# Full-height count products, a three-pass down product, and a reordered opening in a fused embedding, attention and expert kernel

## The reference, cut to what matters

```python
h = concat([cls, patches(x) @ W.T + b]) + pos          # 16 images: 197 rows of 192
h = concat([h, txt], axis=1)                           # + 128 text rows: S = 325
n = layernorm(h); q, k, v = split(n @ W_qkv + b_qkv)
h = h + ((q @ k.T) / sqrt(192) * decay_mask) @ v       # causal 0.99**(i-j), no softmax
n = layernorm(h)                                       # T = 16*325 = 5200 tokens
sig = sigmoid(n @ Wg.T); idx = top_k(sig + e_bias, 6)  # 128 experts, 6 per token
w = 2.5 * sig[idx] / sum(sig[idx])
for e in experts:                                      # the first 192 tokens of each
    g, u = split(n[tokens_e] @ W_gate_up[e])           # 192 -> 2 x 464
    routed[tokens_e] += (silu(g) * u) @ W_down[e] * w  # 464 -> 192
shared = silu(n @ Wsg) * (n @ Wsu) @ Wsd               # 192 -> 928 -> 192, all tokens
out = h + routed + shared
```

## Time and profile before

| | |
|---|---|
| three runs | 699.82, 701.12, 701.90 us; median 701.12 |
| profiled execution | 699.24 us, span 697.4 us |
| busy, share of the span | TensorE 97%, its weight load 91%, VectorE 67%, ScalarE 48%, POOL 29% |
| chain that ended last | TensorE 80%, VectorE 10%, issue 4% |
| images 0 to 15, with the opening | about 0 to 270 us |
| counts and chunks ahead | about 270 to 319 us |
| ten pairs of experts | 318.7 to 672.6 us, 35.4 us each |

### The profile page before, as it was taken

One profiled execution on the slowest core, in us unless ns is written; L12 is line 12 of the kernel. 1 busy time (PEld: TensorE's weight loads), 2 busy tenths in 40 slices (PEclk: granted clock), 3 DMA queues, 4 the chain that ended last, 5 costly groups with the idle time before them and its releaser, 6 DMA issues.

```text
span 697.4 us, 16667 instructions
## 1 busy us (share of the span) xinstructions
PE 678.6 (97%) x4613; PEld 635.5 (91%) x4614; DVE 469.4 (67%) x1490; ACT 332.0 (48%) x803; POOL 201.4 (29%) x309
## 2 busy tenths in 40 slices
PE   6989999999999999999999999999999999999997
PEld 6879988899988888799999999999999999999997
DVE  2357878888788878765666566666675757576653
ACT  2245555565555666444445343434444434343543
POOL 3022223223223210202323233333333242424240
PEclk9899999999999999999999999999999999999999
DMA  7236434545344321733445454545454545454542
GB/s 232 89 99 210 129 112 148 158 154 152 115 137 141 108 95 63 182 61 63 95 103 108 104 103 106 105 106 104 105 107 102 106 102 107 98 108 97 103 88 56
DMA packets 75188, 79.54 MB, mean 114 GB/s; under 512 B 6505, under 2 KB 67065, under 8 KB 75162
## 3 DMA queue, kind: packets, MB, share of 16 engines
q1 hardware_dynamic: 62538, 65.69, 33.9%
q0 software_dynamic: 11760, 12.31, 11.6%
q10 hardware_dynamic: 864, 1.25, 0.6%
HBM read 51.91 MB, written 19.32 MB: 102 GB/s over the span
## 4 chain that ended last, share of the span: by engine, by line
PE 80%; DVE 10%; issue 4%; ACT 2%; DVEq 1%; POOL 1%; POOLq 0%; ACTq 0%
PE bank L1275 24%; PE bank L1243 12%; PE bank L1292 8%; PE bank L1073 8%; PE bank L1255 8%; PE bank L1061 6%; PE bank L1293 4%; PE bank L1103 3%; PE bank L1217 2%; DVE stats L1454 1%; DVE w_raw L1565 1%; PE bank L1131 1%; PE bank L1088 1%; DVE y_B L1474 1%; DVE h L1490 1%
## 5 line engine op out<-in xcount | busy, mean ns | idle before, releaser
L1740 DVE TENSOR_TENSOR s_inter<-s_gate,bank 128x384 f32<-128x384 f32 (+1 forms) x112 | 60.2, 539 | 73.2 <-PE bank L1275 67.0
L906 ACT ACTIVATE s_gate<-bank 128x384 f32<-128x384 f32 (+1 forms) x112 | 53.5, 478 | 79.1 <-PE bank L1275 79.0
L1292 PE MATMUL bank<-s_dn,s_in_hi 128*128 128x384 f32 (+1 forms) x287 | 88.9, 371 | 0.3 <-DVE s_in_lo L1748 0.2
L727 POOL DMA_INDIRECT result<-y_rows,put_idx x40 | 59.8, 1496 | 57.8 <-DVE y_rows L1727 42.1
L1275 PE MATMUL bank<-all_hiA,s_hi 128*128 (+4 forms) x210 | 73.9, 352 | 0.6 <-DVE s_inter L1740 0.6
L1293 PE MATMUL bank<-s_dn,s_in_lo 128*128 128x192 f32 (+1 forms) x287 | 72.9, 254 | 0.0
L1073 PE MATMUL bank<-w_tok,patches 128*128 128x192 f32 x360 | 68.4, 343 | 4.2 <-DMA patches<-xp 4.0
L798 ACT ACTIVATE y<-h,shift,rstd 128x192 f32<-128x192 f32 (+2 forms) x96 | 45.6, 538 | 54.9 <-POOL shift L658 54.9
L1275 PE MATMUL bank<-all_B,s_lo 128*128 (+4 forms) x210 | 70.2, 334 | 0.0
L1275 PE MATMUL bank<-all_B,s_hi 128*128 (+4 forms) x210 | 70.2, 334 | 0.0
L1275 PE MATMUL bank<-all_loA,s_hi 128*128 (+4 forms) x210 | 70.0, 333 | 0.0
(11 more groups left out here) (216 smaller groups left out, 1831.5 us busy)
## 6 DMA issues: line engine op xcount, KB each, us to landing
raw_gu<-wgu SPq DMA_DIRECT2D x22, 464.0 KB, 5.4
raw_gu<-wgu SPq DMA_DIRECT2D x44, 232.0 KB, 6.0
patches<-xp SPq DMA_DIRECT2D x15, 588.0 KB, 4.3
down_w<-wdn SPq DMA_DIRECT2D x22, 348.0 KB
result<-s_rows POOLq DMA_DIRECT2D x12, 288.0 KB
result<-h SPq DMA_DIRECT2D x16, 192.0 KB
yw_rows<-y SPq DMA_DIRECT2D x16, 192.0 KB
all_hiA<-y_hiA SPq DMA_DIRECT2D x16, 162.5 KB, 2.6
```

What stands on the lines that cost most here:

```text
L727: pool.indirect_dma_start(acc[:, :], bass.IndirectOffsetOnAxis(ap=put_idx[:, h:h + 1], axis=0), y_rows[:, h, :], None, compute_op=ALU.add) ...
L906: act.activation(s_gate[m % 2][0:r, 0:width], up_banks(m, alone)[0][0:r, 0:width], ACT.Silu).then_inc(s_gate_ready, 1)
L1292: pe.matmul(bank[0:r, 0:2 * D], s_in_hi[:, m, rows], s_dn[:, m, :], start=m == 0, stop=False)
L1740: dve.tensor_tensor(s_inter[m % 2][0:r, 0:width], s_gate[m % 2][0:r, 0:width], up, ALU.mult).then_inc(s_inter_ready, 1)
```

## The change

- `WARM` is 6 instead of 10. In the opening the transfer of `patches_1` moves from SyncE's queue to ScalarE's, and the text rows of image 0 go ahead of the attention weights.
- ScalarE evacuates `q` of image 0 ahead of normalizing image 1. In `step(0)` VectorE does the residual ahead of splitting image 1's turned rows, and `token_rows(2)` ahead of `values(1)`; TensorE turns image 0's rows ahead of `attend(1)`.
- `counts` and `image` are 128 rows high instead of 16; the rows from 16 on are zeroed once by POOL. The products take all 128 rows.
- The down product is split: `down_part` and `inter_part` on ScalarE, `down_low` and `inter_low` on VectorE, three products in place of one. The low parts overwrite their sources (`raw_gu`, `down_w`, `inter`); so `load_weights` waits for the first layer's products (`gu_mm`) instead of `gu_split`.
- Expert 1's count products move from the second chunk ahead to the third, and expert 0's one `s_up` later.

```diff
-WARM = 10
+WARM = 6
@@ buffers
+        down_hi = [sb(f"down_hi{p}", [F, EM, D], F32R) for p in range(2)]
+        inter_hi = sb("inter_hi", [F, EM, CAP], F32R)
+        gu_lo = [over_raw(f"gu_lo{p}", [128, 2, 2 * I], F32R) for p in range(2)]
+        down_lo = [over_down(f"down_lo{p}", [F, EM, D], F32R) for p in range(2)]
+        inter_lo = Region(inter_at).place("inter_lo", [F, EM, CAP], F32R)
-        counts = [sb(f"counts{p}", [B, SP], BF16) for p in range(2)]
-        image = sb("image", [B, CAP], BF16)
+        counts = [top.place(f"counts{p}", [128, SP], BF16) for p in range(2)]
+        image = top.place("image", [128, CAP], BF16)
@@ sync
+                sp.dma_start(addend[IMG - 128:128, 1, :], txt[0, 0:256 - IMG, :]).then_inc(t1_in, 16)
                 sp.dma_start(first[0:96, 0:2 * QK_COLS], w_first[0:96, 0:2 * QK_COLS]).then_inc(wqk_in, 16)
-                sp.dma_start(addend[IMG - 128:128, 1, :], txt[0, 0:256 - IMG, :]).then_inc(t1_in, 16)
...
-                sp.dma_start(patches_1[:, :, 1:IMG], xp[1, :, :, :]).then_inc(patch_1_in, 16)
...
-                        wait_apart(sp, passed, (gu_split, 4 * j + 2 * n - 2))
+                        wait_apart(sp, passed, (gu_mm, 8 * j + 4 * n - 4))
@@ gpsimd
+                for own in (*counts, image):
+                    pool.memset(own[:, :], 0.0)
...
                 get_tokens(0, 0, True)
+                add_shared(1, 16, *AHEAD[1])
                 get_tokens(0, 1, True)
-                add_shared(1, 16, *AHEAD[1])
@@ scalar
                 act.dma_start(base[:, :, :], c_base).then_inc(base_in, 16)
+                act.dma_start(patches_1[:, :, 1:IMG], xp[1, :, :, :]).then_inc(patch_1_in, 16)
...
-                normed(n1, h0[:, by_turns(1), :], 1)
                 act.wait_ge(qv_lo_set, 1)
                 q_evac(0)
+                normed(n1, h0[:, by_turns(1), :], 1)
...
+                def down_part(j, n):
+                    act.wait_ge(down_in[n % 2], arrivals(j, n, n % 2, 16))
+                    act.activation(down_hi[n % 2][:, :, :], down_w[n % 2][:, :, :], ACT.Copy).then_inc(down_hi_ready, 1)
+                def inter_part(j, n, i):
+                    act.wait_ge(inter_ready, 8 * j + 4 * n + 2 * i + 2)
+                    own = slice(2 * i, 2 * i + 2)
+                    act.activation(inter_hi[:, own, :], inter[:, own, :], ACT.Copy).then_inc(inter_hi_ready, 1)
... together(j) on ScalarE
                     s_silu(o, WIDTH, 2)
+                    inter_part(j, 0, 0)
                     s_hi_part(o, WIDTH, 1)
                     gu_part(j, 1, 1)
                     silu(j, 0, 3)
                     s_silu(o, WIDTH, 3)
+                    inter_part(j, 0, 1)
                     s_hi_part(o, WIDTH, 2)
                     split_x(j, 1)
                     s_silu(o, WIDTH, 4)
                     s_hi_part(o, WIDTH, 3)
+                    down_part(j, 1)
                     silu(j, 1, 0)
...
                     s_silu(o, WIDTH, 7)
+                    inter_part(j, 1, 0)
...
                     split_x(j, 2)
+                    inter_part(j, 1, 1)
                     gu_part(j, 2, 1)
+                    down_part(j, 2)
@@ tensor
-                    if begun:
-                        attend(n + 1)
                     turn(n2, n)
-                    if more and not begun:
+                    if more:
                         attend(n + 1)
...
-                        pe.wait_ge(down_in[n % 2], arrivals(j, n, n % 2, 16))
-                        pe.wait_ge(inter_ready, 8 * j + 4 * n + 4)
+                        pe.wait_ge(down_split, 2 * j + n + 1)
+                        pe.wait_ge(inter_split, 4 * j + 2 * n + 2)
                     for m in range(EM):
-                        mm = pe.matmul(dn_ps[0:CH, h * D:(h + 1) * D], inter[:, m, rows], down_w[n % 2][:, m, :],
-                                       start=m == 0, stop=m == EM - 1)
+                        pe.matmul(ps, inter_hi[:, m, rows], w_hi[:, m, :], start=m == 0, stop=False)
+                        pe.matmul(ps, inter_hi[:, m, rows], w_lo[:, m, :], start=False, stop=False)
+                        mm = pe.matmul(ps, inter_lo[:, m, rows], w_hi[:, m, :], start=False, stop=m == EM - 1)
... ahead of the loop: chunk 1
-                for m in range(2, 5):
+                for m in range(2, 6):
                     s_up(1, data_1, width, m, ALONE)
                 count_rows(0, 0, 0)
-                s_up(1, data_1, width, 5, ALONE)
+                s_up(1, data_1, width, 6, ALONE)
                 count_rows(0, 0, 1)
-                s_up(1, data_1, width, 6, ALONE)
-                count_rows(0, 1, 0)
                 s_up(1, data_1, width, 7, ALONE)
-                count_rows(0, 1, 1)
... chunk 2: count_rows(0, 1, 0) and (0, 1, 1) behind s_up 2 and 3, (0, 2, 0) and (0, 2, 1) behind 5 and 6
@@ vector
-                    if not behind:
-                        split_turned(n + 1)
                     residual(n)
                     residual_stats(n)
-                    if more and behind:
+                    if more:
                         split_turned(n + 1)
                     if behind:
                         choose(n - 1)
+                    else:
+                        token_rows(n + 2)
                     if more:
                         values(n + 1)
-                    if ahead:
+                    if ahead and behind:
                         token_rows(n + 2)
... together(j) on VectorE
                     s_mul(o, WIDTH, 2)
+                    inter_low(j, 0, 0)
                     s_lo_part(o, WIDTH, 1)
                     gu_low(j, 1, 1)
                     gated(j, 0, 3)
                     s_mul(o, WIDTH, 3)
+                    inter_low(j, 0, 1)
                     s_lo_part(o, WIDTH, 2)
                     split_x(j, 1)
...
                     slot_tokens(j, 3)
+                    down_low(j, 1)
                     gated(j, 1, 0)
...
                     s_mul(o, WIDTH, 7)
+                    inter_low(j, 1, 0)
...
                     split_x(j, 2)
+                    inter_low(j, 1, 1)
                     slots(j, 4, 0)
...
                     slot_tokens(j, 4)
+                    down_low(j, 2)
                     s_sum(o, WIDTH, TILES, 2)
```

More of the change, by code:

```diff
@@ L65 @@
 BEHIND = (T - BASE) // WIDTH
+FROM_TOP = 227616
 AHEAD_TILES = sum(t for _, _, t in AHEAD)
@@ L258, in build @@
         sb = experts.place
+        raw_gu_at = experts.at
         raw_gu = [sb(f"raw_gu{p}", [128, 2, 2 * I]) for p in range(2)]
+        down_at = experts.at
         down_w = [sb(f"down_w{p}", [F, EM, D]) for p in range(2)]
@@ L268, in build @@
         gu_hi = [sb(f"gu_hi{p}", [128, 2, 2 * I], F32R) for p in range(2)]
-        gu_lo = [sb(f"gu_lo{p}", [128, 2, 2 * I], F32R) for p in range(2)]
+        down_hi = [sb(f"down_hi{p}", [F, EM, D], F32R) for p in range(2)]
+        inter_hi = sb("inter_hi", [F, EM, CAP], F32R)
+        over_raw = Region(raw_gu_at).place
+        gu_lo = [over_raw(f"gu_lo{p}", [128, 2, 2 * I], F32R) for p in range(2)]
+        over_down = Region(down_at).place
+        down_lo = [over_down(f"down_lo{p}", [F, EM, D], F32R) for p in range(2)]
+        inter_lo = Region(inter_at).place("inter_lo", [F, EM, CAP], F32R)
         lists = Region(max(weights_split.at, from_counts))
@@ L294, in build @@
         y_rows = sb("y_rows", [CH, 2, D])
+        top = Region(FROM_TOP)
+        counts = [top.place(f"counts{p}", [128, SP], BF16) for p in range(2)]
+        image = top.place("image", [128, CAP], BF16)
+        assert max(lists.at, images.at) <= FROM_TOP, (lists.at, images.at)
         added_rows = Region(from_end).place("added_rows", [128, TILES, D])
@@ L1391, in _ @@
                 s_up(2, data, width, 5, ALONE)
+                count_rows(0, 2, 0)
+                s_up(2, data, width, 6, ALONE)
                 count_rows(0, 2, 1)
-                s_up(2, data, width, 6, ALONE)
                 more_k = load_more(pe, act_n)
@@ L1674, in slot_images @@
                     wait(dve, cnt_mm, 4 * j + 2 * n)
-                    own = counts[n % 2]
+                    own = counts[n % 2][0:B, :]
                     dve.tensor_scalar(reach[:, :], rest_row[:, :], own[:, 0:1], None, ALU.is_le).then_inc(reach_ready, 1)
                     dve.wait_ge(reach_ready, 2 * j + n + 1)
-                    dve.scalar_tensor_tensor(image[:, :], rest_row[:, :], own[:, SP - 1:SP], reach[:, :],
+                    dve.scalar_tensor_tensor(image[0:B, :], rest_row[:, :], own[:, SP - 1:SP], reach[:, :],
                                              ALU.is_gt, ALU.mult).then_inc(image_ready, 1)
@@ L1715, in gu_low, with down_low, inter_low @@
                                       ALU.subtract).then_inc(gu_split, 1)
+                def down_low(j, n):
+                    dve.wait_ge(down_hi_ready, 2 * j + n + 1)
+                    dve.tensor_tensor(down_lo[n % 2][:, :, :], down_w[n % 2][:, :, :], down_hi[n % 2][:, :, :].bitcast(F32),
```

(17 more changed lines are left out.)

27 lines of the change are left out of this document (16 added, 11 removed).

## The result

The changed kernel takes 683.08 us (median of four runs, 681.10 to 685.45), beside 700.47 for the kernel before on the same chip: ratio 0.975, 95% interval 0.9725 to 0.9775. Forecast were 680.3 us and 672 to 691. The profiled execution took 681.10, 2.7 us more than the 678.4 of the sum.

What follows compares the result with a forecast made beforehand. TensorE's issue time bounds the pair loop, waits the opening and phase change. Terms -7.0 (loop), -12.2 (opening), -1.6 (phases) sum to -20.8: 699.24 to 678.4, plus 1.9 for the median: 680.3 us, range 672 to 691.

Steps and rivals of the forecast that it cites:

- Height: Pair loop: full-height count products lose the gap, 0.15 instead of 0.44 us each, saving 1.16 us per pair.
- the six early ones: Count products before the pair loop: 1.7 us would be lost there if the gap stayed.
- Down product: Pair loop: three fp32r passes take 1.08 us per half, saving 0.91 per pair, but stall the first expert 1.07.
- rival D: Pair loop: the later `raw_gu` load lands late and holds back ScalarE and TensorE; 704 us at 3.0 late; chance 3%.
- The 0.3 for the second expert: Pair loop: added VectorE subtractions delay `s_mul` 5, so `s_up` 6 and 7 start late; 0.3 us per pair.
- Opening's first part: Opening: shorter warm-up and earlier `patches_1` let image 1 run 12.7 to 16.7 at full clock; -6.5 us.
- their own weights' arrival isn't shown: Opening: products of the attention weights gain only 0.3 us, ending at 12.7 instead of 12.99.
- rival B: Opening stays cold: warm-up doesn't raise the clock or the transfer isn't early, image 1 at 0.50; 687 us; chance 12%.
- the normalized image 0: Opening: the next late item after image 1's tokens, expected about 16.9, its text rows 0.8 us earlier.
- Query copy, step 0, clock: Opening: earlier query copy -1.1, reordered step 0 -3.0, no clock drop behind the removed waits -1.6 us.
- Change of phases: From images to experts: count gaps and waits go, down product waits about 1.7, even chance of clock drop; -1.6 us.
- Tokens of image 1 at half clock: Opening: a sign that would prove the sum wrong; expected were these tokens before 13.5 at clock 1.0.

Runs made afterwards that it cites:

- the low counts: The changed kernel with the count products over 16 rows again: 695.64 us, ratio 0.9935.
- the fp32 kernel: The changed kernel with the experts' down product back in fp32, without the splits of weights and gated values: 679.36 us, ratio 0.9706.
- the swap: The changed kernel with the attention weights ahead of image 0's text rows on SyncE's queue: 679.42 us, ratio 0.9725.
- step 0 undone: The changed kernel with the old order of step 0, query copy behind the normalization of image 1 included: 687.32 us, ratio 0.985.
- the fastest kernel: The changed kernel with attention weights ahead of text rows, six products of zeros before image 1's tokens, and a later first down half: 676.97 us, ratio 0.9691.
- text on ScalarE: The changed kernel with image 0's text rows on ScalarE's queue, between patch weights and base rows: 682.83 us, ratio 0.9751.

## Why the prediction was right, and where it wasn't

**Height: right.** 0.29 per product forecast, 0.29 measured in the loop. For the six early ones it had 1.7 us, and they cost 0.5 when undone. Of the two rules cited from the Trainium skill the first (TensorEngine Tiling (Array Packing), Key Properties) is the one this case bears out. The second (TensorE: Matmul & The Clock Gate, "Why this matters for your kernels") is on a lone product of 32 rows, and doesn't hold for one of 16 between two full ones: 0.44 us with 16 rows, 0.12 with 128.

**Down product: sizes right, the sum not.** 1.07 per half against 1.08, the wait 1.17 by the starts against 1.07, no wait for the later `raw_gu` (rival D). The 0.3 for the second expert doesn't show as a wait: in the loop TensorE waits ten times for `inter_lo` (10.1 us) and for nothing else. Net I had +4.6 us; the runs show +3.7 with the low counts and +0.7 with the high ones. The difference between the two is that with high counts and no wait for `inter_lo`, TensorE waits for VectorE elsewhere: I added the two edits as if they didn't share VectorE. Both orders lead to -7.9. So in this kernel the three-pass down product is a small loss, and the counts make the whole gain of the loop.

**Opening's first part: wrong, -1.5 (22.46 beside 23.98) for -6.5.** Two steps failed. The first: "their own weights' arrival isn't shown, so I let them gain only 0.3: 12.7." `patches_1` was there by 13.5, near the 13.0 forecast. But the weights landed at 13.1, since the change puts the text rows ahead of them, which the prediction gives no price. TensorE idled 2.09 us, the clock fell, and all of image 1 went at half. In part that is rival B, by a cause it didn't name. It costs 2.3: the fp32 kernel, with the same opening, waited 0.97 and 2.35 us, kept 1.00 and had the turn at 20.13. Of the seven kernels profiled with the text rows ahead on SyncE's queue and nothing in the wait, one kept the clock; of the three executions with the swap (one with zeros in the wait), all did. I can't say what decides between them.

The second failed step is the normalized image 0, "about 16.9 (its text rows arrive 0.8 earlier than now)". In every kernel that kept the clock the turn still waits for it, until 19.83 to 20.19 (the bracket `<-ACT y` above), 2.6 us behind the 17.5 that the sum implies. This is ScalarE's normalization, before and after:

```profile
16.23 1.42 ACT L798 ACTIVATE y<-h,shift,rstd 128x192 f32<-128x192 f32 x3 [2.64 <-POOL shift L658]
```
```profile
18.44 1.42 ACT L816 ACTIVATE y<-h,shift,rstd 128x192 f32<-128x192 f32 x3 [1.35 <-POOL shift L673]
```

It is 2.2 us later and not earlier. The last 69 text rows of image 0 land at 14.5 instead of 12.3, and at 12.8 with `patches_1` back on SyncE: most of that is the price of moving `patches_1`. So about half of the 5.0 us that are missing is the late weights with the clock, and half is this; even an opening at full clock would have given 3.9 and not 6.5. A third reading was wrong without a cost: the third part of image 0's patches lands at 9.4 us (9.1 in the kernel before) and not by 5.8, so image 0 ends at 11.0 and not at 9.5, and the wait for the weights hides it.

**Query copy, step 0, clock: the sum right, 5.9 for 5.7.** 4.3 of it are the three waits, shown by undoing. The remaining 1.6 fits the clock's 1.6 (the earlier trace rows have 0.70 in 52 to 55; the tokens there took 3.13 us and now take 2.16), but the clock didn't fall again when the waits returned. So the step "with those waits gone the clock should not fall behind them" isn't confirmed, and the cause of this part stays open.

**Change of phases: near, -2.3 for -1.6, but with a wait I had missed.** The clock, an even chance in the sum, stayed at 1.00 from 270 to 309 us, where it had been 0.72 for a time. `down_low(0,0)` needs the first down weights, and VectorE stands behind it. After, then step 0 undone:

```profile
288.44 0.96 DVE L1753 TENSOR_TENSOR down_lo<-down_w,down_hi 116x768 fp32r<-116x768 f32 x1 [2.95 <-ACT down_hi L911]
```
```profile
294.38 0.96 DVE L1755 TENSOR_TENSOR down_lo<-down_w,down_hi 116x768 fp32r<-116x768 f32 x1 [4.47 <-ACT down_hi L911]
...
296.48 0.41 PE L1312 MATMUL bank<-all_hiA,s_hi 128*128 128x384 f32 x1 [1.15 <-DVE s_inter L1787]
```

These are waits of VectorE for ScalarE, which in turn waits for the transfer. Behind the one of 2.95 us TensorE doesn't wait, behind the one of 4.47 it does: the stretch takes 67.6 us after, 69.3 there, and 68.8 in the fastest kernel (4.1 us of that wait). Why the weights land later against the work there isn't shown.

**Sum.** Too much by 5.0 in the opening's first part, too little by 0.2, 0.7, 0.9 and 0.4 in the others: 2.8 in all. The prediction named "Tokens of image 1 at half clock" as a proof that its sum is wrong. That came true: the total is near because four smaller errors went the other way, which is luck. One sum in it is off by itself: rival D at 3.0 us late gives 680.3 + 25 = 705, not 704.

## What to carry to other kernels

Before you move a transfer, list every one that now stands behind another on its queue, small ones above all, and every one on the other queue that now runs beside it, and ask for each whether its landing is shown. When two engines are close to each other's pace, a stall taken from one place of an order shows up at the next: price the edit by the idle time of the slower queue, not by the stall. In one ordered queue, add two edits' gains only after asking which third engine both lean on.

## What the runs showed of the hardware

**A small transfer of 59 rows delays what is behind it by more than its size.** Image 0's text rows (59 rows of 768 bytes, 44.2 KB) ahead of the weights (338.2 KB) on SyncE's queue, with `patches_1` on ScalarE's: 9.6 to 10.5 us to landing in seven kernels; behind them or on the other queue: 7.1 to 7.7 in five. With `patches_1` on SyncE's queue the difference is smaller, 9.2 beside 8.2. Ahead of `base` and `patches_1` on ScalarE's queue: 9.8 and 13.2 instead of 7.2 and 10.6. The delay follows the transfer from one queue to the other.

The traces show more of it than the rows above. They hold a landing signal for each part of a transfer: sixteen for the weights (96 rows), `base` and `patches_1`, but one for the 59 text rows and three for the 69 rows of `h`, beside one at once after the issue. Times of these signals in us:

| transfer | the kernel | most parts by | the late ones |
|---|---|---|---|
| weights, behind the text rows | changed | 14 by 9.2 | 10.9, 13.1 |
| weights, ahead of them | swap | 14 by 9.3 | 10.0, 10.2 |
| `base` and `patches_1`, no text rows ahead | changed | 15 by 9.4 and 12.4 | 9.5 and 13.5 |
| the same, behind the text rows | text on ScalarE | 15 by 9.5 and 12.3 | 12.7 and 16.5 |
| 59 text rows | changed | none | 11.8 |
| 69 rows of `h` | changed | 2 by 10.7 | 14.5 |

So the small transfer moves in one part, and what is queued behind it is late in one part of sixteen, by 2 to 4 us behind the last but one, while the others are on time. That the late part waits in line behind the text rows is the plain reading of the table; the traces don't say which part goes where. Not tested: a shape of the text rows that moves in sixteen parts.

**The same idle time costs the clock or doesn't.** 2.6 us of waiting in two parts were followed by 0.50 (the changed kernel), 3.3 us in two parts by 1.00 (fp32 down product), 2.5 and 2.75 us in two parts by 1.00 (the swap, two executions). 2.3 us hang on it: in kernels with the wait for the weights, single executions differ by that much and more, and their mean granted clock goes with it (fp32 down product: 677.46 and 678.15 us at 0.999 and 0.997, 680.58 and 681.01 at 0.995; the changed kernel: 681.10 and 681.69 at 0.995, 684.47 and 685.45 at 0.992). The five timed together with the swap alone lie within 1.3 us, at 0.997 to 1.000. So a profile of one execution says little about this stretch.
